# Small block-diagonal products in a chunked scan: from two 64x64 squares of the array to four 32x32 squares

## The reference

```
sa = einsum('bhij,bhj->bhi', s, a_)
s  = s * w_[:, :, None, :] + sa[..., None] * b_[:, :, None, :] + v_[..., None] * k_[:, :, None, :]
y  = einsum('bhij,bhj->bhi', s, q_)
```

## Time and profile before

| | us |
|---|---|
| median of 3 runs (lowest, highest) | 5692.52 (5689.09, 5694.93) |
| the profiled execution | 5688.41 |
| its span, first to last instruction | 5686.6 |
| scan: TensorE's loop, 60 turns | 1038.9 to 2221.2 |
| scan: unrolled rest | 2221.2 to 2306 |

### The profile page before, as it was taken

One profiled execution on the slowest core, in us unless ns is written; L12 is line 12 of the kernel. 1 busy time (PEld: TensorE's weight loads), 2 busy tenths in 40 slices (PEclk: granted clock), 3 DMA queues, 4 the chain that ended last, 5 costly groups with the idle time before them and its releaser, 6 DMA issues. The chain is left out here.

```text
span 5686.6 us, 196589 instructions
## 1 busy us (share of the span) xinstructions
PE 5261.2 (93%) x71072; PEld 4544.2 (80%) x71072; DVE 3823.9 (67%) x11245; ACT 3328.7 (59%) x9386; POOL 2621.4 (46%) x3584
## 2 busy tenths in 40 slices
PE   6888887899999998659999999999799999999999
PEld 5888886899999998547777777777667777777777
DVE  4666665799999998546666666666366666666665
ACT  4777776355555555436666666666355555556665
POOL 1222222899999998003333333333243444444443
PEclk8999998999999999879999999999899999999999
DMA  2333333676766765660000000000100000000000
GB/s 76 93 93 93 93 93 94 142 149 146 151 141 147 150 144 125 194 206 13 14 14 14 14 14 14 14 14 14 46 14 20 20 20 20 18 19 20 20 20 17
DMA packets 993634, 387.34 MB, mean 68 GB/s; under 512 B 773872, under 2 KB 938608, under 8 KB 992624
## 3 DMA queue, kind: packets, MB, share of 16 engines
q1 hardware_dynamic: 992304, 384.91, 28.2%
q10 hardware_dynamic: 1088, 0.00, 0.0%
HBM read 216.46 MB, written 168.30 MB: 68 GB/s over the span
## 5 line engine op out<-in xcount | busy, mean ns | idle before, releaser
L1828 POOL TENSOR_TENSOR l_pn<-l_prob,l_rinv 128x512 f32<-128x512 f32 x512 | 532.3, 1040 | 1278.0 <-DVE l_rinv L1928 1273.5
L2146 ACT ACTIVATE l_prob<-l_prob,l_nb,l_rq 128x256 f32<-128x256 f32 x1024 | 604.4, 591 | 287.6 <-DVE l_nb L1948 287.1
L1841 POOL TENSOR_TENSOR l_outt<-l_t,l_xat 128x256 f32<-128x256 f32 x64 | 46.5, 726 | 554.0 <-DVE l_t L2010 554.0
L1089 POOL TENSOR_TENSOR sc_kT<-sc_tok,sc_headmask 128x128 f32<-128x128 f32 x512 | 298.6, 602 | 0.0
L1197 ACT ACTIVATE sc_d_qk<-sc_part,sc_headmask 128x64 f32<-128x64 f32 x1024 | 270.2, 336 | 38.8 <-DMA sc_part<-scratch_part 38.8
L1089 POOL TENSOR_TENSOR sc_bT<-sc_tok,sc_headmask 128x128 f32<-128x128 f32 x512 | 277.8, 561 | 0.0
L475 POOL TENSOR_TENSOR rk<-rk,bkraw 128x256 f32<-128x256 f32 x64 | 54.6, 872 | 477.8 <-DVE bkraw L361 477.8
L1197 ACT ACTIVATE sc_d_qb<-sc_part,sc_headmask 128x64 f32<-128x64 f32 x1024 | 271.8, 339 | 0.0
L1127 PE MATMUL sc_AB<-sc_early,sc_bx 64*64 64x64 f32 x4096 | 172.4, 220 | 41.8 <-POOL sc_kx L1068 35.1
L470 POOL TENSOR_TENSOR xm<-tm,h 128x512 f32<-128x512 f32 x64 | 75.5, 1180 | 281.9 <-DVE tm L313 281.9
L1068 POOL TENSOR_TENSOR sc_ax<-sc_late,sc_headmask 128x256 f32<-128x256 f32 x256 | 168.0, 656 | 80.4 <-PE sc_Y L1135 78.0
(11 more groups left out here) (359 smaller groups left out, 17984.6 us busy)
## 6 DMA issues: line engine op xcount, KB each, us to landing
scratch_cm<-cm SPq DMA_DIRECT2D x64, 512.0 KB, 4.1
sc_early<-scratch_cm SPq DMA_DIRECT2D x128, 256.0 KB, 3.3
scratch_part<-sc_att SPq DMA_DIRECT2D x64, 512.0 KB, 4.5
sc_part<-scratch_part SPq DMA_DIRECT2D x64, 512.0 KB, 4.3
scratch_tok<-vt SPq DMA_DIRECT2D x512, 48.0 KB, 1.8
l_h<-scratch_h SPq DMA_DIRECT2D x128, 129.0 KB, 2.6
scratch_gr<-gr SPq DMA_DIRECT2D x64, 256.0 KB, 2.0
sc_late<-scratch_cm SPq DMA_DIRECT2D x64, 256.0 KB, 3.8
```

Source lines behind the costliest of these rows:

```text
L1089: last = nc.gpsimd.tensor_tensor(dst[c][:, b * CC:(b + 1) * CC], tok[k][:, c, b, x].unsqueeze(2).broadcast_to([P, CC, HQ, HS]), headmask[: ...
L1828: tt(pn[s][:, pair], prob[s][:, pair], rinv[s][:, pair].unsqueeze(2).broadcast_to([P, 2, 2 * P]), ALU.mult).then_inc(Q["pn"][s].sem, 1)
L2146: last_ = nc.scalar.activation(prob[s][:, h], prob[s][:, h], ACT.Exp, scale=rq8[s][:, h:h + 1], bias=nb[s][:, h:h + 1], accum_out=sums[s][ ...
```

## The change

`QH` becomes 32, so `HQ` is 2: a stationary operand holds two heads instead of four, and `headmask` is [P, 2]. Each tile of block-diagonal operands has half the columns, and ScalarE's `diagonal` issues 2 copies instead of 4. TensorE issues one matmul for each of four 32-row slices instead of two 64-row halves, each on the diagonal 32x32 square named by `tile_position`. The moving operand is passed without the broadcast: 16 columns in `stacked`, 32 in `products`. The results lie packed in the bank, and the readers take them without a stride.

```diff
-QH = 64
+QH = 32
...
-        first16 = lambda bank: bank[:].rearrange("p (q r i) -> p q r i", q=BG, i=HS)[:, :, 0, :]
+        stacked_out = lambda bank: bank[:, 0:BG * HS].rearrange("p (q i) -> p q i", q=BG)
...
-                halves = (slice(0, QH), slice(QH, P))
+                tiles = tuple(slice(at, at + QH) for at in range(0, P, QH))
...
-                            for at in halves:
-                                rhs = early[c // 2][at, c % 2, 0, q // CC, q % CC].unsqueeze(1).broadcast_to([QH, 2, 2, CH])
-                                last = mm(bank[at, q * P + x * QH:q * P + (x + 1) * QH], src[c % 2][at, q].rearrange("p h t -> p (h t)"),
-                                          rhs, start=True, stop=True)
+                            for at in tiles:
+                                rhs = early[c // 2][at, c % 2, 0, q // CC, q % CC].rearrange("p y t -> p (y t)")
+                                last = mm(bank[at, (2 * q + x) * 2 * CH:(2 * q + x + 1) * 2 * CH], src[c % 2][at, q].rearrange("p h t -> p (h t)"),
+                                          rhs, start=True, stop=True, tile_position=(at.start, at.start))
...
-                        for at in halves:
-                            ins = mm(bank[at, q * P:q * P + QH], lhs[at, q].rearrange("p h t -> p (h t)"),
-                                     rhs[at, q].unsqueeze(1).broadcast_to([QH, HQ, HS]), start=first and q == 0, stop=last_,
-                                     skip_group_check=True)
+                        for at in tiles:
+                            ins = mm(bank[at, q * HS:(q + 1) * HS], lhs[at, q].rearrange("p h t -> p (h t)"), rhs[at, q],
+                                     start=first and q == 0, stop=last_, skip_group_check=True, tile_position=(at.start, at.start))
...
-                    nc.scalar.copy(p_sb[:], first16(P_ps)).then_inc(S["p_sb"].sem, 1)
+                    nc.scalar.copy(p_sb[:], stacked_out(P_ps)).then_inc(S["p_sb"].sem, 1)
...
-                                            AB_ps[c % 2][:].rearrange("p (z r n) -> p z r n", z=2 * BG, n=2 * CH)[:, :, 0, :],
+                                            AB_ps[c % 2][:, 0:4 * BG * CH].rearrange("p (z n) -> p z n", z=2 * BG),
```

More of the change, by code:

```diff
@@ L1236, in chunk @@
                     act.wait_ge(S["y_ps"].sem, S["y_ps"].after(n, 1))
-                    nc.scalar.copy(sa_sb[:], first16(SA_ps)).then_inc(S["sa_sb"].sem, 1)
+                    nc.scalar.copy(sa_sb[:], stacked_out(SA_ps)).then_inc(S["sa_sb"].sem, 1)
                     if follow:
@@ L1243, in chunk @@
                         act.wait_ge(Hf["sum"][k].sem, Hf["sum"][k].after(w, 1))
-                    nc.scalar.copy(y[k][:, c], first16(Y_ps[c % 2])).then_inc(S["y_sb"].sem, 1)
+                    nc.scalar.copy(y[k][:, c], stacked_out(Y_ps[c % 2])).then_inc(S["y_sb"].sem, 1)
                 act.preload_act_table_set(LN_EXP)
@@ L1385, in chunk @@
                     dve.wait_ge(S["s_sb"].sem, S["s_sb"].after(n, 1))
-                    nc.vector.tensor_tensor(s_sum[:], first16(S_ps), state[c % 2][:], ALU.add).then_inc(S["s_sum"].sem, 1)
+                    nc.vector.tensor_tensor(s_sum[:], stacked_out(S_ps), state[c % 2][:], ALU.add).then_inc(S["s_sum"].sem, 1)
                     dve.wait_ge(S["s_sum"].sem, S["s_sum"].after(n))
```

## The result

Median of 4 runs 7324.62 us (7310.56 to 7348.07), against 5690.81 us for the kernel before beside it (4 runs, 5688.46 to 5694.93): 1.287 times as long, 95% interval 1.284 to 1.291, 1634 us more. The prediction was 7660 us, range 6200 to 8350. The profiled execution is the longest of the four, 7348.07 us.

The account below looks back on a forecast made before the run. TensorE was taken to bound the kernel, its longer loop body refetched every turn: 12 x 4.3 = 51.6 us a turn, loop +1914, unrolled rest +57, on 5688 us giving 7660 us. Range 6200 to 8350; the forecast's own, 7000 to 8350.

Parts of the forecast that it names:

- What bounds the kernel before, and the count of instructions: Scan loop: TensorE sets the pace at 19.7 us a turn; matmuls and loads grow from 1280 to 2560 a turn.
- The body doesn't stay, and 12 fetches a turn: TensorE's scan loop: the new body of 10.2 blocks is refetched every turn, 11 blocks plus a wait at the branch.
- The price of a fetch: TensorE's code in the scan: 4.3 us per block of 256 instructions, between 3.8 and about 5.0.
- (b): Rival: body fits, but TensorE instructions issue no closer than 14.6 ns; 38.1 us a turn, 6830 us; chance 0.07 with (d).
- (c): Rival: TensorE's code refetched back to back at 2.5 us a block, 30 us a turn, +620, 6310 us; chance 0.05.
- a thirteenth fetch: Upper end of the range: one more code fetch in each scan turn, 8190 us becoming some 8350.
- (a): Rival: TensorE's code comes in time or fits; VectorE bounds the scan, 3.9 us a chunk, -247, 5440 us; chance 0.17.
- The overlap of four squares: Scan products: four 32x32 squares overlap fully, a group of 32 records taking about 0.25 us, 2.5 us a chunk.
- (d): Rival: the scan's squares don't overlap, 40 us a turn, below the fetches' 51.6; chance 0.07 together with (b).
- the fast rival: Another name for rival (a): code free of charge, VectorE bounding the scan, 5440 us; chance 0.17.
- Everything else hidden: Halved expansions and copies on VectorE, GpSimd and ScalarE lie beside TensorE, costed at nothing while TensorE sets the pace.

Follow-up runs that it names:

- before_two_units: Kernel before with its products untouched, only TensorE's loop body doubled to two units (8 chunks) and 30 turns instead of 60; 6160.45 us, 1.082 times before.
- after_2planes: Kernel after with two of the four planes of products in TensorE's loop, half of the scan's products there left out; 5571.96 us, 0.979 times before.
- half_body: Kernel after with all its work, TensorE's loop body cut to 2 chunks (120 turns), buffers of period 2, last chunks looped too; 5674.34 us, 0.997 times before.
- after_3planes: Kernel after with three of the four planes of products in TensorE's loop, a quarter of the scan's products there left out; 6808.82 us, 1.197 times before.
- half_body_32: half_body with the 16-column moving operand of the products by `stacked` repeated once, to 32 columns; 5610.31 us, 0.986 times before.
- before_narrow: Kernel before with its 64x64 squares, only the repeated columns of the moving operand taken away; 6576.97 us, 1.155 times before.
- after_wide: Kernel after, four 32x32 squares, with the columns of the moving operand repeated to 64 again; 7364.78 us, 1.293 times before.
- half_body_wide: half_body with all moving operands repeated to 64 columns on each 32x32 square; 5704.86 us, 1.002 times before.
- after_hint: Kernel after with one instruction more, a hint at the top of TensorE's loop naming the branch at its end; 7225.27 us, 1.269 times before.

## Why the prediction came out as it did

**What bounds the kernel before, and the count of instructions: right.** 75535 matmuls and 75527 loads in 59 turns are 1280 of each a turn, as counted.

**The body doesn't stay, and 12 fetches a turn: right, to the packet.** 12.0 a turn, and 33 in the rest where 33 blocks were counted. before_two_units shows that length alone does it; after_2planes and half_body, that a short body has none. The chain is: twice the instructions, a body that no longer stays, a stop at each block, TensorE late, all others waiting for it.

**The price of a fetch: the mis-sized term.** I took 4.3 us from a stretch of the unrolled rest and it measured 46.77 / 12 = 3.90 us. Over 720 fetches this makes 720 x 0.4 = 288 us, nearly all of the miss. There a block also issued for 3.7 us, and here one issues in 2.1; that this makes the difference is likely and not shown (see the last section). The full account of the profiled execution against rows of before: loop 60 x 46.77 - 1182.3 = +1624 (forecast +1914); rest 131 us, 3833.9 to 3965.0, against 85 (+46; forecast +57); the loop's start, counted back from its end, 11 us earlier (forecast nothing). The sum, +1659 us, is the difference of the two spans, 7346.3 - 5686.6 = 1659.7. The median of the runs lies 23 us below this execution. The range, 6200 to 8350 us, also holds rivals (b) and (c), so the time alone would have decided little; the packets, the stops and before_two_units decide. Its upper end is also summed wrongly: a thirteenth fetch at 5.0 us adds 60 x 5.0 = 300 us to the 8190, and not 160. The result is far below either.

**Refetched back to back at 2.5 us, rival (c): wrong**, except at the branch, where two packets do follow within 0.4 us and the stop is still 5.0 us. **Rival (a), free of charge: denied** by 12 packets a turn. The rule that the Trainium skill states (Runtime: NRT & Kernel Launch, Instruction fetch mechanics), 2048 instructions for PE, would have let the three-plane body of some 1970 stay; after_3planes shows 9.0 fetches a turn. The same section's "mostly hidden" is denied by the 2.1 to 2.5 us stops above.

**The overlap of four squares: right, at the wrong clock.** 0.25 us a group was forecast. The kernel after never shows it, since its clock is halved: records start 13.3 ns apart on average in its bursts, 53.3 ns for a square, a group 0.43 us. Four squares one after the other would be 32 x 53.3 ns = 1.7 us a group, so (d) is denied. half_body_32 comes to 0.28 us where the clock is up. **Rival (b), instructions no closer than 14.6 ns: denied** as well, by 0.43 / 32 = 13.3 ns in the kernel after and 0.28 / 32 = 8.8 ns in half_body_32. On one square, though, starts are 35 ns apart even there, so these runs say nothing of how close they can come on a single square.

**Not foreseen: the clock.** The prediction priced the dropped columns as pure gain. before_narrow prices them by themselves, on two squares, at +882 us. It did no harm to the number because the fetches lie over it (after_wide: the same time at clock 0.76), but in the fast rival it would have: even with 163 KB in reach, ten groups of 0.43 us take 4.3 us a chunk, above the 3.9 on which the 5440 us of (a) rest. half_body, where no fetch is left, takes 5674 us.

**Everything else hidden: right** for the halved expansions and copies, whose engines are idle for over two thirds of the loop. What would come next I named wrongly: not VectorE at 3.9 us a chunk but TensorE's half clock and, where that is lifted, the load of v and VectorE's wait for the store of y.

## What to carry to other kernels

Before a product is split into smaller ones, count the instructions of the engine's loop body, not only the work in them: here 5.8 blocks of 256 stayed and 7.7 did not, and past that each fetch of a block cost 3.9 to 4.6 us on every turn, whatever the products took. Look at the granted clock before repeated or padded columns are called waste; the best width (32 here) lay between the one that repeats nothing and the one that holds the clock fully. A long gap on "issue" that falls every 256 instructions, with packets on the engine's instruction queue, is code and not a semaphore; a shorter body removes it. Here that took buffers of a shorter period, and the frame had its own price, 70 us with two squares.

## What the runs showed of the hardware that I had not expected

- The granted clock stayed at 0.50 with TensorE busy in 1000.00 of 1000.00 us (before_narrow), and stood at 1.00 with 969 of 1000 at 64 columns (half_body_wide). The trace gives the clock that was granted, not why.
- At the lower clock, 16 and 32 columns cost the same: a group of 32 records on four squares takes 0.43 us in half_body (16 columns) and in half_body_32 (32 columns). Two 64x64 squares take 0.86 us for 16 records with 16 columns (before_narrow), twice the time for half the records.
- A fetch's period grew with what else went on: 3.9 us in the kernel after, 4.2 in after_3planes, 4.6 in before_two_units, where the DMA share is 0.30, 0.36 and 0.50 and a block's issue some 2.1, 2.1 and 3.7 us. Which of the two does it was not separated and stays open; the stretch of the kernel before with 4.3 us at a share of 0.16 and the long issue speaks against the traffic as the only cause. The exact size that stays, between 5.8 and 7.7 blocks, is open too.
- A back-edge hint saves one of the 12 packets and 2.1 us a turn, no more (after_hint).
